# Three fp32r passes for part of the `wq × s` product in a 12-layer attention and FFN kernel on Trainium2

## The reference

```python
for i in range(12):                                 # H = 16 heads of D = 8
    qkv = x @ Wqkv[i].T + bqkv[i]
    q, k, v = split and reshaped to B, H, T, D
    att = einsum('bhqd,bhkd->bhqk', q, k) * scale   # no softmax
    y = einsum('bhqk,bhkd->bhqd', att, v)
    x = y @ Wproj[i].T + bproj[i] + x
x = layernorm(x0 + x)
gate, up = x @ wg.T, x @ wu.T                       # 128 -> 384
x = layernorm(x + (silu(gate) * up) @ wd.T)
```

## Time and profile before

| | before |
|---|---|
| median of 3 runs (lowest, highest) | 320.84 us (320.58, 322.96) |
| profiled execution | 319.78 us |
| its span in the profile | 318.0 us |
| PE busy | 306.1 us, 96% |
| DVE busy | 222.9 us, 70% |
| ACT busy | 182.6 us, 57% |
| POOL busy | 96.1 us, 30% |
| chain that ended last | PE 93%, DVE 3%, DMA 1% |
| one layer, start of n to start of n (122.36 less 101.87) | 20.49 us |

### The profile page before, as it was taken

The page is one execution under the profiler, slowest core; times in us unless marked ns, Lnnn a source line. Parts: engine busy times, 40 slices in busy tenths (PEclk is TensorE's granted clock), DMA queues, the critical chain, the costliest instruction groups (busy, mean ns, idle before and its releaser), DMA issues.

```text
span 318.0 us, 8958 instructions
## 1 busy us (share of the span) xinstructions
PE 306.1 (96%) x3754; PEld 284.9 (90%) x3754; DVE 222.9 (70%) x639; ACT 182.6 (57%) x418; POOL 96.1 (30%) x90
## 2 busy tenths in 40 slices
PE   8999999999999999999999999999999999999993
PEld 8989899899898998989989989899898788999882
DVE  0367776875776767767667577676776877888874
ACT  2438758376484674855748658377485055544450
POOL 3015055060320601405006042060236052665443
PEclk9999999999999999999999999999999999999998
DMA  7942002020020200200102002020000000111112
GB/s 279 334 167 76 6 6 72 2 78 2 2 76 3 77 1 5 76 4 14 65 2 79 2 2 76 4 77 2 2 1 3 2 2 0 35 46 56 33 33 72
DMA packets 7594, 14.93 MB, mean 47 GB/s; under 512 B 512, under 2 KB 4736, under 8 KB 7424
## 3 DMA queue, kind: packets, MB, share of 16 engines
q1 hardware_dynamic: 6976, 13.27, 12.5%
q10 hardware_dynamic: 576, 1.06, 0.9%
HBM read 12.23 MB, written 2.10 MB: 45 GB/s over the span
## 4 chain that ended last, share of the span: by engine, by line
PE 93%; DVE 3%; DMA 1%; issue 1%; POOLq 0%; POOL 0%
PE ps L868 14%; PE ps L815 13%; PE ps L901 13%; PE ps L767 7%; PE ps L765 7%; PE ps L1002 7%; PE ps L766 7%; PE ps L834 4%; PE ps L991 4%; PE ps L990 4%; DVE s_rows L603 3%; PE ps L854 3%; PE ps L783 2%; PE ps L968 2%; PE ps L841 2%; PE ps L826 2%
## 5 line engine op out<-in xcount | busy, mean ns | idle before, releaser
L366 POOL TENSOR_TENSOR step_lo<-step,step_hi 128x512 fp32r<-128x512 f32 x44 | 54.9, 1280 | 171.8 <-ACT step_hi L447 171.8
L765 PE MATMUL ps<-state_hi,step_hi 128*128 128x258 f32 x176 | 50.7, 288 | 0.0
L868 PE MATMUL ps<-s_rows,w 32*128 32x256 f32 x768 | 44.8, 380 | 5.3 <-DVE s_rows L603 5.3
L767 PE MATMUL ps<-state_hi,step_lo 128*128 128x258 f32 x176 | 49.9, 283 | 0.0
L766 PE MATMUL ps<-state_lo,step_hi 128*128 128x258 f32 x176 | 49.6, 282 | 0.0
L868 PEld LDWEIGHTS ps<-s_rows,w 32*128 32x128 f32 x768 | 40.4, 185 | 7.2 <-ACT s_rows L441 7.2
L447 ACT CAST step_hi<-step 128x512 fp32r<-128x512 f32 x44 | 27.0, 619 | 33.7 <-DVE step L609 33.7
L815 PE MATMUL ps<-w,gram 128*128 128x128 f32 x352 | 42.8, 275 | 0.0
L815 PEld LDWEIGHTS ps<-w,gram 128*128 128x128 f32 x352 | 42.0, 192 | 0.6
L901 PE MATMUL ps<-step,gram 128*128 128x128 f32 x320 | 40.6, 281 | 0.0
L901 PEld LDWEIGHTS ps<-step,gram 128*128 128x128 f32 x320 | 37.3, 192 | 3.3 <-DVE step L609 3.3
(11 more groups left out here) (112 smaller groups left out, 478.4 us busy)
## 6 DMA issues: line engine op xcount, KB each, us to landing
w<-weights SPq DMA_DIRECT2D x12, 592.5 KB, 3.7
xchan<-x_chan SPq DMA_DIRECT2D x1, 2048.0 KB, 10.7
out<-xchan SPq DMA_DIRECT2D x7, 256.0 KB, 2.3
xt<-x_tok ACTq DMA_DIRECT2D x4, 258.0 KB, 5.4
xt<-x_tok SPq DMA_DIRECT2D x4, 258.0 KB, 5.1
fw_int<-ffn_weights SPq DMA_DIRECT2D x1, 576.0 KB, 4.9
out<-xchan SPq DMA_DIRECT2D x2, 128.0 KB, 1.8
cst<-consts SPq DMA_DIRECT2D x1, 147.0 KB, 7.1
```

Source lines behind the costliest of these rows:

```text
L366: nc.gpsimd.tensor_tensor(group(step_lo, g), group(step, g), group(step_hi_f, g), ALU.subtract).then_inc(step_lo_ready, 1)
L765: nc.tensor.matmul(dst, l_hi, r_hi, start=True, stop=False)
L767: return nc.tensor.matmul(dst, l_lo, r_hi, start=False, stop=True)
L868: last = nc.tensor.matmul(n_banks(h)[:, k, :], w[r, s, WQ + P * i:WQ + P * (i + 1)], s_rows[r, h, i, :], start=i == 0, stop=i == QUADS - 1)
```

## The change

- **n, second half** (h = 1): the four quads are three fp32r passes each, `wq_hi·s_hi`, `wq_lo·s_hi` and `wq_hi·s_lo`, of four matmuls. ACT casts the high parts out of PSUM (two casts, into `s_hi`), DVE subtracts the low parts (two, into `s_lo`).
- **n, first half** (h = 0): quads 0 to 2 stay float32; the last quad is three fp32r passes. GpSimd casts the quad from `s_rows` (`s_quad_hi`) and subtracts (`s_quad_lo`).
- **wq**: in every layer ACT casts `wq_hi` (128×512) after its last copy of gk, and GpSimd subtracts `wq_lo`.
- **bias products**: `bqp` moves from DVE to GpSimd, after `split_quad`; the sum `mbq` on DVE moves from ahead of `add_identity(0)` to behind `add_identity(1)`. In layer 12 the new work on GpSimd stands between the sums of B.
- **low flag**: its 1×1 product moves from the shift stage of layer 3 to the gk stage of layer 4, and DVE's read of it ahead of `kdiag`.
- **start**: six products on zeros, and the first transfer of x is split in two halves, one on each queue.
- **last chunk**: the down products of tokens 0 and 1 run as early as they can; the half of tokens 2 and 3 follows.

The diff, cut to its core (semaphores, the moved 1×1 product and the removed lines of the old down stage's neighbours are left out):

```diff
-WARM_START = 7
+WARM_START = 6
...
+        s_rows = sb("s_rows", [P, QUADS, 2 * P])
+        s_quad_hi = sb("s_quad_hi", [P, 2 * P], F32R)
+        s_quad_lo = sb("s_quad_lo", [P, 2 * P], F32R)
+        s_hi = sb("s_hi", [P, QUADS, 2 * P], F32R)
+        s_lo = sb("s_lo", [P, QUADS, 2 * P], F32R)
+        wq_hi = sb("wq_hi", [P, QUADS * P], F32R)
+        wq_lo = sb("wq_lo", [P, QUADS * P], F32R)
...
-            for i in range(0, PAIRS, 2):
+            sp.dma_start(xt[:, x_first[0], :], x_v[:, x_first[0], :]).then_inc(x_in[0], 16)
+            for i in range(1, PAIRS, 2):
...
+                def low_of_wq():
+                    pool.wait_ge(wq_hi_ready, at(1, 1))
+                    nc.gpsimd.tensor_tensor(wq_lo[:, :], w[:, s, WQ:WQ + QUADS * P], wq_hi[:, :].bitcast(F32),
+                                            ALU.subtract).then_inc(wq_lo_ready, 1)
+
+                def split_quad():
+                    pool.wait_ge(s_high_half_ready, at(1, 1))
+                    nc.gpsimd.tensor_copy(s_quad_hi[:, :], s_rows[:, QUADS - 1, :]).then_inc(s_quad_hi_ready, 1)
+                    pool.wait_ge(s_quad_hi_ready, at(1, 1))
+                    nc.gpsimd.tensor_tensor(s_quad_lo[:, :], s_rows[:, QUADS - 1, :], s_quad_hi[:, :].bitcast(F32),
+                                            ALU.subtract).then_inc(s_quad_lo_ready, 1)
+
+                def sum_of_b(g):
+                    nc.gpsimd.tensor_tensor(group(bsum, g), state_hi_f[:, GB * g:GB * (g + 1), S_B:S_B + P],
+                                            state_lo_f[:, GB * g:GB * (g + 1), S_B:S_B + P],
+                                            ALU.add).then_inc(bsum_ready, 1)
+
+                def bq_products():
+                    pool.wait_ge(m_ready, at(GROUPS, GROUPS))
+                    nc.gpsimd.tensor_tensor(bqp[:, :, :], mt[:, :, :],
+                                            w[:, s, BQ:BQ + QUAD].unsqueeze(1).to_broadcast([P, BATCHES, QUAD]),
+                                            ALU.mult).then_inc(bqp_ready, 1)
...
                 if last:
 
                     pool.wait_ge(b_lo_ready, at(PAIRS, PAIRS))
                     pool.wait_ge(kdiag_ready, at(1, 1))
-                    for g in range(GROUPS):
-                        nc.gpsimd.tensor_tensor(group(bsum, g), state_hi_f[:, GB * g:GB * (g + 1), S_B:S_B + P],
-                                                state_lo_f[:, GB * g:GB * (g + 1), S_B:S_B + P],
-                                                ALU.add).then_inc(bsum_ready, 1)
+                    sum_of_b(0)
+                    low_of_wq()
+                    sum_of_b(1)
+                    split_quad()
+                    bq_products()
+                    sum_of_b(2)
+                    sum_of_b(3)
                     return
 
+                low_of_wq()
+                split_quad()
+                bq_products()
...
-            for i in range(1, PAIRS, 2):
+            act.dma_start(xt[:, x_first[1], :], x_v[:, x_first[1], :]).then_inc(x_in[0], 16)
+            for i in range(2, PAIRS, 2):
                 act.dma_start(xt[:, per * i:per * (i + 1), :], x_v[:, per * i:per * (i + 1), :]).then_inc(x_in[i], 16)
...
-                for h in range(2):
-                    act.wait_ge(s_done, at(2, h + 1))
-                    nc.scalar.copy(s_rows[:, h, 0:2, :], s_banks(h)[:, 0:2, :]).then_inc(s_low_half_ready, 1)
+                act.wait_ge(w_in[s], at(8, 16 - 8 * s))
+                if not first:
+                    act.wait_ge(n_done, at(2, 0))
+                nc.scalar.copy(wq_hi[:, :], w[:, s, WQ:WQ + QUADS * P]).then_inc(wq_hi_ready, 1)
+                act.wait_ge(s_done, at(2, 1))
+                nc.scalar.copy(s_rows[:, 0:2, :], s_banks(0)[:, 0:2, :]).then_inc(s_low_half_ready, 1)
+                act.wait_ge(s_done, at(2, 2))
+                for i in range(0, QUADS, 2):
+                    nc.scalar.copy(s_hi[:, i:i + 2, :], s_banks(1)[:, i:i + 2, :]).then_inc(s_hi_ready, 1)
                 if last:
                     return
...
-                def take_s(h):
-                    dve.wait_ge(s_done, at(2, h + 1))
-                    nc.vector.tensor_copy(s_rows[:, h, 2:4, :], s_banks(h)[:, 2:4, :]).then_inc(s_high_half_ready, 1)
+                def take_s():
+                    dve.wait_ge(s_done, at(2, 1))
+                    nc.vector.tensor_copy(s_rows[:, 2:4, :], s_banks(0)[:, 2:4, :]).then_inc(s_high_half_ready, 1)
+
+                def low_of_s(i):
+                    dve.wait_ge(s_hi_ready, at(2, i // 2 + 1))
+                    nc.vector.tensor_tensor(s_lo[:, i:i + 2, :], s_banks(1)[:, i:i + 2, :], s_hi[:, i:i + 2, :].bitcast(F32),
+                                            ALU.subtract).then_inc(s_lo_ready, 1)
...
-                take_s(0)
-                take_s(1)
-
-                dve.wait_ge(m_ready, at(GROUPS, GROUPS))
-                nc.vector.tensor_tensor(bqp[:, :, :], mt[:, :, :],
-                                        w[:, s, BQ:BQ + QUAD].unsqueeze(1).to_broadcast([P, BATCHES, QUAD]),
-                                        ALU.mult).then_inc(bqp_ready, 1)
+                take_s()
+                low_of_s(0)
+                low_of_s(2)
+
+                add_identity(0)
+                add_identity(1)
                 dve.wait_ge(bqp_ready, at(1, 1))
                 nc.vector.tensor_reduce(mbq[:, :], bqp[:, :, :], AX_X, ALU.add).then_inc(mbq_ready, 1)
-                add_identity(0)
-                add_identity(1)
                 if not last:
                     add_identity(2)
                     add_identity(3)
 
                 def take_shift():
                     dve.wait_ge(shift_done, at(1, 1))
-                    if at(1, 0) == LOW_LAYER:
-                        nc.vector.tensor_scalar(low_flag[:, :], ps[0:1, SHIFT_BANK, BATCHES:BATCHES + 1], 1.0, None,
...
-                    pe.wait_ge(s_low_half_ready, at(2, h + 1))
-                    pe.wait_ge(s_high_half_ready, at(2, h + 1))
+                    if h == 0:
+                        pe.wait_ge(s_low_half_ready, at(1, 1))
+                        pe.wait_ge(s_high_half_ready, at(1, 1))
+                    else:
+                        pe.wait_ge(s_lo_ready, at(2, 2))
+                        pe.wait_ge(wq_lo_ready, at(1, 1))
                     for i in range(QUADS):
-                        for k in range(QUADS):
-                            r = slice(QUAD * k, QUAD * (k + 1))
-                            last = nc.tensor.matmul(n_banks(h)[:, k, :], w[r, s, WQ + P * i:WQ + P * (i + 1)],
-                                                    s_rows[r, h, i, :], start=i == 0, stop=i == QUADS - 1)
+                        quad = slice(P * i, P * (i + 1))
+                        f32 = w[:, s, WQ + P * i:WQ + P * (i + 1)]
+                        s_parts = (s_hi[:, i, :], s_lo[:, i, :]) if h else (s_quad_hi[:, :], s_quad_lo[:, :])
+                        if h or i == QUADS - 1:
+                            parts = ((wq_hi[:, quad], s_parts[0]), (wq_lo[:, quad], s_parts[0]), (wq_hi[:, quad], s_parts[1]))
+                        else:
+                            parts = ((f32, s_rows[:, i, :]),)
+                        for p, (left, right) in enumerate(parts):
+                            if h == 0 and len(parts) > 1:
+                                pe.wait_ge(wq_lo_ready, at(1, 1))
+                                pe.wait_ge(s_quad_lo_ready if p == 2 else s_quad_hi_ready, at(1, 1))
+                            for k in range(QUADS):
+                                r = slice(QUAD * k, QUAD * (k + 1))
+                                last = nc.tensor.matmul(n_banks(h)[:, k, :], left[r, :], right[r, :],
+                                                        start=i == 0 and p == 0, stop=i == QUADS - 1 and p == len(parts) - 1)
                     last.then_inc(n_done, 1)
...
-                first, final = ((0, CT // 2), (CT // 2 - 1, CT - 1)) if last_chunk else ((0,), (CT - 1,))
-                for j in range(HC):
+
+                def products_of(j, tokens, first=(), final=()):
                     pe.wait_ge(hid_ready, n * HC + (HC + j + 1))
-                    for t in range(CT):
+                    for t in tokens:
                         bank = HT_BANK if last_chunk and t >= CT // 2 else DOWN_BANK
                         last = nc.tensor.matmul(ps[:, bank, P * t:P * (t + 1)], hid[:, j, P * t:P * (t + 1)],
...
+                                                wd[:, j, :], start=t in first, stop=t in final)
+                    return last
+
+                if last_chunk:
+
+                    products_of(0, (0, 1, 2), first=(0, 2))
+                    products_of(1, (0, 1))
+                    products_of(2, (0, 1), final=(1,)).then_inc(down_done, 1)
+                    products_of(0, (3,))
+                    products_of(1, (2, 3))
+                    products_of(2, (2, 3), final=(3,)).then_inc(down_done, 1)
+                else:
```

(41 more changed lines are left out.)

3 lines of the change are left out of this document (1 added, 2 removed).

## The result

| | before | with the change |
|---|---|---|
| median (lowest, highest) | 320.71 (319.69, 322.96) us, 4 runs | **316.91** (316.45, 317.53) us, 4 runs |
| ratio of the two | | 0.988, 95% interval 0.984 to 0.992 |
| profiled execution, its span | 319.78, 318.0 | 316.45, 314.6 |
| n to n, sixth layer | 20.49 | 20.16 |

The kernel is 1.2% faster: 3.8 us by the medians, 3.3 by the two profiled executions; 317.6 was forecast. The fourth execution of before (319.69) came with the result, so its median is 320.71 here and not 320.84. Of all the executions in this document three took far longer (759 us with the bias product on DVE, 618 and 442 of the kernel before) and are left out of the comparisons.

A forecast was written before the change was run, and what follows sets the result against it. PE was taken to bound the kernel, with DVE's `step`s setting H's start after the change. Terms of −3.3, +0.75, +0.15, −0.15 and −0.64 made −3.2 us, from a median of 320.84 to 317.6 us, range 315.0 to 320.6.

The forecast's parts named there:

- What H waits for: Eleven layers: DVE's second `step` sets H's start, 125.74 against 126.03; 0.3 us a layer, −3.3 us in all.
- The wait for DVE: Before H in each layer: the last 0.15 us of what PE saves in n is lost waiting for DVE.
- The pass on four row groups: n on PE: an fp32r group takes 0.117 us, between 0.107 and 0.13, making n 0.41 us shorter.
- rival C: n's four row groups overlap less in fp32r: 0.139 a group, 319.8 us (8%); no overlap, 370 us (2%).
- The new operands: Casts and subtractions on ACT, DVE and GpSimd arrive in time for n; GpSimd's quad has 0.4 us in hand.
- Rivals A and B: A: GpSimd's quad or `s_lo` chain late, 320.4 us (20%). B: GpSimd's narrow operations cost like wide ones, 331 us (9%).
- Layer 12: GpSimd's quad 0.45 us late among the sums of B, then PE's shift product waits for `mbq`: +0.75 us.
- The moved 1×1 product: In gk of layer 4 it costs PE the same, and DVE's `kdiag` comes about 0.15 us late: +0.15.
- The last chunk: Tokens 0 and 1 end with the 14th record instead of the 20th, so DVE's y starts earlier: −0.64 us.
- The start: x's split transfer lands some 0.3 us earlier, half counted: −0.15 us, not below −0.3; up to 1.7 lost if slow pace lasts.
- The sum: Whole kernel: −3.3 + 0.75 + 0.15 − 0.15 − 0.64 = −3.2 us, giving 317.6 us.

## Why the prediction was right, point by point

- **What H waits for.** Right, and the centre of it: `step` (0) 1.97 after n was worked out and 1.97 measured; H at 3.38 after n, 3.32 measured, as DVE's semaphore reaches PE in 0.05 and not in 0.11. That is 0.35 a layer instead of 0.30, over eleven layers 0.6 of the 0.77 by which the gain of the layers was forecast too small (3.15 against 3.92); the rest is the 1×1 product below. The wait for DVE was sized too large as well: n's last group of four starts 3.31 after n before and 3.03 with the change, which with a group's own time of 0.216 and 0.12 makes n 0.38 shorter (0.41 forecast), and 0.35 of it arrives at H. Only 0.03 was lost in the wait, not 0.11 to 0.15. That a still shorter half 1 brings nothing more, the run with one pass showed.
- **The pass on four row groups.** Taken at 0.117, measured 0.118 (half 1's twelve: 122.56 to 123.86, eleven steps). The rival C, 0.139 by 3.07× in the Trainium skill, "TensorE: Matmul & The Clock Gate", Measured speedup vs the span model, isn't borne out here, at 256 columns where the page's figure is for 512: half the pace of the float32 groups would be 0.108, so the fp32r groups overlap to within 10% as well as those.
- **The new operands.** The cast 0.40 (0.4 taken, from bounds far apart; the 0.3 worked out beside it was too low), the subtraction 0.73 (0.69), in time by 0.37 (0.4 said). Rivals A and B didn't come; A was near, as one more subtraction put the period above that of the kernel before.
- **Layer 12.** +0.78 (0.75), by the mechanism given: the quad late (0.46), then `mbq` behind the two `step`s (0.32). What it didn't see was `nu_part`, 0.12 us longer beside GpSimd.
- **The moved 1×1 product.** +0.15 was forecast; that layer's period is 20.47 against 20.16 of its neighbours, before 20.82 against 20.5. It cost nothing new.
- **The last chunk.** −0.61 (−0.64).
- **The start.** The term with the wrong sign: −0.15 was forecast, +0.27 measured. x did land earlier, by more than I said (PE starts on it at 3.77, before at 4.59), but I took the moment of the faster pace as fixed. It lay anywhere from 4.1 to 7.3 us in 14 profiles, and the range of the term (−0.3 to +1.7) took that in.
- **The sum.** It came out 0.2 us too small in the gain, but part of that closeness is luck: an error of +0.4 at the start, itself a draw, hid more than half of the −0.77 in the layers.

## What to carry to other kernels

When a stage on the bounding engine is to be made shorter, work out from the rows which other engine releases the next stage, with its semaphore: the gain is what moves that release, and here 0.35 of n's saving counted while 0.96 more counted for nothing. A DVE operation with two inputs in SBUF that the chain hangs on should not start while a long GpSimd operation runs, however narrow it is. And at a gain of 1%, compare stretches of two profiles that start behind the noisy part, not only the times.

## What the runs showed of the hardware that was not expected

- **DVE held up by GpSimd.** `nu_part` (128×16, two SBUF inputs) took 1.26 us when it started just behind a GpSimd sum of 1.27, 0.29 when it started in the last quarter of one, and 0.18 with GpSimd idle; both times it ended 0.03 us behind the end of that one sum. In the kernel before DVE's `bqp`, 0.68 in the other layers, took 1.33 in layer 12, where it started in the middle of a sum (`bqp` ends 0.55 behind the sum). It goes the other way as well: with the bias product on DVE, GpSimd's sum took 1.74 instead of 1.27. DVE's operations with one input from PSUM (`s_lo`, `step`) kept their 0.69 beside GpSimd. This agrees with the Trainium skill, "GPSIMD Engine Reference", 8. Key points, on contention with DVE instructions that have two SBUF inputs. The rows give the size: the wait is the rest of the one operation that runs. The kernel before, then the change:

```profile
245.35 1.27 POOL L359 TENSOR_TENSOR gram_raw<-state_hi,state_lo 128x512 f32<-128x512 f32 x1
245.84 1.33 DVE L619 TENSOR_TENSOR bqp<-mt,w 128x512 f32<-128x512 f32 x1
...
245.95 1.27 POOL L385 TENSOR_TENSOR gram_raw<-state_hi,state_lo 128x512 f32<-128x512 f32 x1
246.96 0.29 DVE L606 TENSOR_TENSOR nu_part<-shift,mu 128x16 f32<-128x16 f32 x1
```

- **PE without instructions, perhaps.** In layer 1 of the six profiles above PE stood still inside n for 0.27 to 1.10 us at a stretch with nothing in the rows but "issue". In those profiles the instruction queue's first transfer of that stretch began at 18.2 to 19.2 us from the start, in the others at 15.2 to 17.4 (once, with one pass in half 1, at 18.2 with H only 0.19 late), while the last transfer of x (2 MB) kept the DMA engines busy. The order of the two was seen each time; that the one causes the other was not tried.
- **The slow pace at the start** ended 4.1 to 7.3 us after the start, though PE had worked from 1.05 with no idle time over 0.2 us. The trace's own table of the granted clock has no record before that moment, and its first record is at the higher of the two levels (2.4 GHz): at 5.27 us before, at 6.88 with the change, at 4.03 with seven zero products the second time, in each of the 14 profiles 0.01 to 0.12 us ahead of the first fast record. The windows of a profile print the clock as full for the earlier stretch too, though the pace there is the slow one. What sets the moment stays open.
